# A causal attention block on one core: one decision on the score bound, read behind the tail, in place of one before each chunk with two code paths

## The chip, the core and the metric

The program runs on one core of a Trainium2 chip. The metric is the device time of one execution in microseconds. The core has five engines with an instruction list each: PE (TensorE, matmuls and transposes), DVE (VectorE), ACT (ScalarE), POOL (GpSimd) and SP (SyncE, which issues every DMA here). They meet at semaphores.

## The reference

One transformer block on 2048 tokens of width 256, all in float32:

```python
x = x + attn(layernorm(x))       # 16 heads of 16, causal, softmax over up to 2048 keys, o_proj
x = x + ffn(layernorm(x))
# ffn: x @ W.T + b, plus a LoRA update of rank 16 from the top 2 of 8 experts,
#      picked by x @ gate_w.T + gate_b, weighted by the softmax of the two logits
```

The softmax is exact for any input. The kernel leaves out the subtraction of the row maximum where it can show that no exponential overflows. For that it bounds every score by the largest squared norm of a query head times the largest squared norm of a key head. With the inputs used here the bound always holds, so the general path, with row maxima, is never run in any time of this document.

## The kernel before, in words

The tokens are cut into 16 tiles of 128 and four chunks of 512 queries. TensorE projects q, k and v of each tile. q and k are split into a float16 high and low part, stored to DRAM and loaded back as stacks (`load_queries`, `load_keys`), in which one matmul of 64 rows gives an exact enough score.

The attention is one list of 272 units, each of 128 keys by two halves of 512 queries. A unit is four or fewer score matmuls (`scores_of`, L741), one exponential of ScalarE (L846), and for the diagonal blocks one mask of VectorE (`clear_later_keys`, L1062). Groups of units are multiplied by the values (`values_of`, L758). Chunk c takes units `FIRST_UNIT[c]` on: 0, 20, 72 and 156. Two units and what belongs to them are a step; the chunks begin at steps 0, 10, 36 and 78, and steps 136 and 137 hold only the last four value groups. There are three score banks, so unit u needs the exponential of unit u - 3.

Between the units, `place_pieces` puts the pieces of other work into the steps: the projection of the next chunk's tiles (turn_x, project_qk L612, project_v L618), the norms of the chunk (norm_q, norm_k, L624) and what follows attention for the tiles of earlier chunks (turn_sums to lora, with the FFN at L669). In chunk 0 a step has two slots for pieces, later one. Every engine goes through the same steps in the same order, and a piece on TensorE waits until the bank of the piece before it has been read (`bank_read`). The last four tiles go through `TAIL_ORDER` when attention is over.

The first chunk's projections are outside the loop (`project_first_chunk`). It ends with the norms of chunk 0 on TensorE (`sum_squares`), their maxima on VectorE (`read_norm`), the seven small steps of `decide_bound` (L1006 to L1019, ending in the flag `is_bounded`), and the transpose of tile 4 on TensorE, which waits for one norm read. `decide_bound` runs again in norm_k of each chunk, for chunk c over the norms of all chunks so far.

Before each chunk TensorE, VectorE and SyncE wait for that chunk's decision, load the flag into a register and branch. TensorE's list holds the steps of each chunk twice, once for either path:

```python
bounded = pe.value_load(is_bounded[0:1, c:c + 1], min_val=0, max_val=1)
with pe.If(bounded == 1):
    for s in range(FIRST_STEP[c], FIRST_STEP[c + 1]):
        step(s, False)
with pe.If(bounded == 0):
    ...
        step(s, True)
```

The second block is jumped over at the end of each chunk, chunk 3 included, ahead of steps 136 and 137. SyncE's list in order: the inputs, the stores and stack loads of chunk 0, the loads of the rest (L435 to L441), then per chunk the decision and, at each project_qk, six stores (`store_parts`) and behind the chunk's last tile the 16 stack loads of the next chunk.

Of the kernel before, what the change touches and what calls it, by code (L numbers as in the profile page):

```python
# [37 lines left out]
PAIRS = H // 2  # L38

# [83 lines left out]
def place_pieces():  # L123
# [78 lines left out]
def transformer_block(nc, x, wqkv, wo, wffn, lora_b, biases, ident, masks, head_sum, expert_ids, ones, out):  # L202
    ctx = ExitStack()
    with ctx:
# [6 lines left out]
        def sem(name):  # L211
# [6 lines left out]
        shift_dram = nc.dram_tensor("shift_dram", (NCHUNK, H, TPC, P), F32, kind="Internal").ap()  # L218
# [8 lines left out]
        masks_sb = sb("masks_sb", [P, 2, P])  # L227
# [20 lines left out]
        squares = sb("squares", [P, 2 * KH, CHUNK], BF16)  # L248
# [6 lines left out]
        is_bounded = sb("is_bounded", [1, NCHUNK], I32)  # L255
# [13 lines left out]

        k32 = k_stack[:].rearrange("p c a t -> p (c a t)").bitcast(F32).rearrange("p (i t) -> p i t", t=S)  # L270
        q32 = [q_stack[:, b].rearrange("p a s -> p (a s)").bitcast(F32).rearrange("p (i t) -> p i t", t=CHUNK)
               for b in range(2)]
        row_max = sb("row_max", [P, 8])
        masked = sb("masked", [P, P])
        shift = sb("shift", [P, TPC])
        shift_out = sb("shift_out", [P, TPC])
        shift_rows = sb("shift_rows", [TPC, P])
# [56 lines left out]
        gen_loaded = [sem(f"gen_loaded{c}") for c in range(NCHUNK)]  # L334
        gen_scores = [sem(f"gen_scores{c}") for c in range(NCHUNK)]
        gen_step = [sem(f"gen_step{c}") for c in range(NCHUNK)]
        gen_read = [sem(f"gen_read{c}") for c in range(NCHUNK)]
        gen_max = [sem(f"gen_max{c}") for c in range(NCHUNK)]
        gen_turned = [sem(f"gen_turned{c}") for c in range(NCHUNK)]
        gen_rows = [sem(f"gen_rows{c}") for c in range(NCHUNK)]  # L340
        gen_out = [sem(f"gen_out{c}") for c in range(NCHUNK)]
        gen_pair = [sem(f"gen_pair{c}") for c in range(NCHUNK)]
        gen_in = [sem(f"gen_in{c}") for c in range(NCHUNK)]
# [50 lines left out]
        tail = [AfterAttention(carver(k32[:, t]), True) for t in range(TPC)]  # L394
        tail_banks = [scores[0][:, 0], scores[0][:, 1], scores[1][:, 0], scores[1][:, 1]]
        tail_turn_banks = [scores[2][:, 0, 0:P], scores[2][:, 1, 0:P], aux[:, 0:P], acc[:, 0:P]]

# [3 lines left out]
        def bank_of(g):  # L401
            return aux[:] if g < TILES - TPC else tail_banks[g - (TILES - TPC)]

        def turn_bank_of(g):
            return aux[:, 0:P] if g < TILES - TPC else tail_turn_banks[g - (TILES - TPC)]

        def sums_of_tile(g, q):
            t = g % TPC
            return sums[:, g // TPC % 3, q, t * P:(t + 1) * P]

# [12 lines left out]
        def _(sp):  # L423
# [6 lines left out]
            sp.dma_start(masks_sb[:], masks).then_inc(consts_in, 16)  # L430
# [55 lines left out]
            def load_general(c):  # L486
                sp.wait_ge(first_qk32_out, 16 * 2 * KH)
                if c > 0:
                    sp.wait_ge(scores_ready, FIRST_UNIT[c])
                    for b in range(2):  # L490
                        sp.wait_ge(qk32_out[b], 16 * 2 * c)
                rows = qk32_dram.rearrange("c k m (j d a) t -> c k m j d a t", j=2, d=DK)
# [33 lines left out]
            for c in range(NCHUNK):  # L526
# [13 lines left out]
                for s in range(FIRST_STEP[c], FIRST_STEP[c + 1]):  # L540
                    for slot in range(2):
# [12 lines left out]
                        if name == "lora":  # L554
                            store_result(n)
# [728 lines left out]
```

## Time and profile before

| | us |
|---|---|
| median of 3 runs (lowest, highest) | 413.61 (411.25, 413.66) |
| the profiled execution | 415.72 |
| its span, first to last instruction | 413.9 |
| busy: PE, ACT, DVE, POOL | 363.4, 279.8, 213.3, 47.8 |
| mean granted clock of TensorE | 0.950 of full |
| scores of chunk 0, 1, 2, 3 begin | 24.15, 71.58, 141.70, 245.46 |
| last value groups begin | 383.36 |

The profile comes from one execution. Times are microseconds from the start of the span. In the timeline an entry is a run of like instructions: when it starts, how long it takes, how many, and in brackets how long its engine was idle before it and what released it. "issue" means that the profile shows nothing that the engine waited for. The granted clock is a share of TensorE's full 2.4 GHz; 0.50 is its lower level.

### The profile page before, as it was taken

How to read it: one execution, taken by the hardware profiler on the slowest of the kernel's cores; microseconds unless marked ns; L12 is line 12 of the kernel's file. 1: busy time of each engine (PE TensorE's matmuls, PEld its weight loads, DVE VectorE, ACT ScalarE, POOL GpSimd, SP SyncE). 2: the span in 40 equal slices, each digit the busy share in tenths (PEclk: the TensorE clock that was granted, in tenths of full speed). 3: DMA queues.
4: the chain of work that ended last, by engine and by line, in shares of the span. 5: the costliest groups of instructions: out<-in, count | busy, mean ns of one | idle time of the engine just before them, and what ended most of it. 6: DMA issues, size and time to landing. Idle time of an engine off the chain costs nothing.

```text
span 413.9 us, 7036 instructions
## 1 busy us (share of the span) xinstructions
PE 363.4 (88%) x2558; PEld 142.1 (34%) x2558; DVE 213.3 (52%) x734; ACT 279.8 (68%) x317; POOL 47.8 (12%) x75
## 2 busy tenths in 40 slices
PE   7966975899998799999999979998997999797884
PEld 3544621445332254423323223233322323211542
DVE  4647565354766535555555444546446344402385
ACT  2524345767887777788788856888787588799121
POOL 5000100001011100011121111211121111100050
PEclk9988869899999999999999999999999899899896
DMA  6578335022350021261000000000000000000001
GB/s 197 159 253 258 82 103 157 18 60 78 89 169 13 3 53 51 74 194 52 14 1 15 13 5 13 2 14 0 14 13 2 13 2 13 14 0 4 3 1 51
DMA packets 29390, 23.51 MB, mean 57 GB/s; under 512 B 15392, under 2 KB 25888, under 8 KB 29344
## 3 DMA queue, kind: packets, MB, share of 16 engines
q1 hardware_dynamic: 29344, 22.91, 18.6%
q8 instruction: 28, 0.46, 0.5%
q14 instruction: 18, 0.15, 0.1%
HBM read 12.41 MB, written 10.49 MB: 55 GB/s over the span
## 4 chain that ended last, share of the span: by engine, by line
PE 63%; DVE 18%; issue 8%; ACT 8%; POOL 2%; DMA 1%; ACTq 0%; DVEq 0%
PE acc L758 23%; PE scores L741 12%; PE aux L612 7%; ACT probs L846 7%; PE aux L669 5%; PE aux L653 3%; PE aux L682 2%; DVE probs L1062 2%; PE aux L618 2%; PE aux L638 1%; DVE ffn L1109 1%; POOL exp_gap L1217 1%; DVE parts L977 1%; DVE gates L1137 1%; PE aux L661 1%
## 5 line engine op out<-in xcount | busy, mean ns | idle before, releaser
L846 ACT ACTIVATE probs<-scores 128x1024 f32<-128x1024 f32 x272 | 260.5, 1031 | 86.1 <-PE scores L741 74.9
L758 PE MATMUL acc<-probs,v_aug 128*32 128x512 f32 (+3 forms) x1280 | 149.5, 555 | 3.3 <-DVE probs L1062 2.4
L741 PE MATMUL scores<-q_stack,k_stack 64*128 64x512 f16 (+3 forms) x640 | 87.3, 357 | 15.6 <-issue 12.1
L741 PEld LDWEIGHTS scores<-q_stack,k_stack 64*128 64x128 f16 x640 | 21.1, 95 | 116.5 <-ACT probs L846 78.8
L1062 DVE TENSOR_TENSOR probs<-probs,masks_sb 128x512 f32<-128x512 f32 (+1 forms) x80 | 44.2, 579 | 23.9 <-ACT probs L846 23.3
L758 PEld LDWEIGHTS acc<-probs,v_aug 128*32 128x32 f32 x1280 | 31.8, 111 | 54.6 <-issue 34.9
L612 PE MATMUL aux<-xT,wqkv_sb 128*128 128x128 f32 x192 | 28.8, 311 | 1.0 <-DVE xT L964 1.0
L612 PEld LDWEIGHTS aux<-xT,wqkv_sb 128*128 128x128 f32 x192 | 26.4, 221 | 5.7 <-issue 3.2
L975 DVE CAST parts<-qk 128x512 f16<-128x512 f32 x12 | 5.1, 427 | 39.9 <-ACT qk L838 39.9
L1206 POOL TENSOR_TENSOR rstd<-ve,minus_half 128x1 f32<-128x1 f32 x12 | 7.3, 608 | 112.2 <-DVE ve L955 112.2
L669 PE MATMUL aux<-wffn_sb,yT 128*128 128x392 f32 x48 | 20.0, 543 | 0.0
L1211 POOL TENSOR_TENSOR rstd<-ve,minus_half 128x1 f32<-128x1 f32 x12 | 6.6, 549 | 106.3 <-DVE ve L1093 106.3
L1109 DVE COPY ffn<-aux 128x392 f32<-128x392 f32 x12 | 6.8, 567 | 22.8 <-PE aux L669 22.8
L1086 DVE TENSOR_TENSOR y<-aux,x_sb 128x256 f32<-128x256 f32 x12 | 5.1, 425 | 23.9 <-PE aux L653 23.9
L1217 POOL TENSOR_TENSOR exp_gap<-euler,top_gap 128x1 f32<-128x1 f32 x12 | 6.6, 550 | 90.3 <-DVE top_gap L1122 90.3
L1067 DVE COPY sums<-acc 128x512 f32<-128x512 f32 x16 | 11.0, 687 | 10.3 <-PE acc L758 10.2
L618 PE MATMUL aux<-wqkv_sb,xT 128*128 128x256 f32 x48 | 13.6, 405 | 1.2 <-ACT qk L838 1.0
L1159 DVE TENSOR_TENSOR result<-aux,yb 128x256 f32<-128x256 f32 x12 | 5.1, 425 | 17.7 <-PE aux L682 17.7
L1098 DVE TENSOR_SCALAR yln<-y,mv,rstd 128x256 f32<-128x256 f32 x12 | 9.7, 810 | 8.0 <-POOL rstd L1211 8.0
L653 PE MATMUL aux<-wo_sb,attn_t 128*128 128x256 f32 x48 | 13.6, 405 | 0.0
L838 ACT COPY qk<-aux 128x512 f32<-128x512 f32 x12 | 7.0, 585 | 9.4 <-PE aux L612 9.4
L676 PE MATMUL aux<-ident_sb,gated 128*128 128x128 f32 x12 | 3.9, 326 | 9.1 <-DVE attn_t L1080 8.2
(148 smaller groups left out, 328.1 us busy)
## 6 DMA issues: line engine op xcount, KB each, us to landing
q_stack<-q_dram SPq DMA_DIRECT2D x32, 128.0 KB, 2.8
k_stack<-k_dram SPq DMA_DIRECT2D x32, 128.0 KB, 2.8
qk_dram<-qk SPq DMA_DIRECT2D x12, 256.0 KB, 2.5
x_sb<-x SPq DMA_DIRECT2D x3, 512.0 KB, 6.8
q_dram<-parts SPq DMA_DIRECT2D x12, 128.0 KB, 2.0
k_dram<-parts SPq DMA_DIRECT2D x48, 32.0 KB, 1.9
out<-result SPq DMA_DIRECT2D x12, 128.0 KB, 1.7
qk_dram<-probs SPq DMA_DIRECT2D x4, 256.0 KB, 3.4
```

Of the source, the lines that this page charges most:

```text
L612: m = pe.matmul(aux[:, n * P:(n + 1) * P], wqkv_sb[:, k, col:col + P], xT[:, k, :], start=(k == 0), stop=(k == KH - 1))
L618: m = pe.matmul(aux[:, 0:D], xT[:, k, :], wqkv_sb[:, k, 2 * D:3 * D], start=(k == 0), stop=(k == KH - 1))
L653: m = pe.matmul(bank_of(g)[:, 0:D], w.attn_t[:, k, :], wo_sb[:, k, :], start=(k == 0), stop=(k == KH - 1))
L669: m = pe.matmul(bank_of(g)[:, 0:FFN], w.yT[:, k, :], wffn_sb[:, k, :], start=(k == 0), stop=(k == KH - 1), skip_group_check=True)
L741: m = pe.matmul(to, k_stack[row:row + STACK, kb // TPC, 2 * i + p, kb % TPC * P:(kb % TPC + 1) * P], q_stack[row:row + STACK, c % 2, 2 * i ...
L758: m = pe.matmul(acc[32 * hp:32 * hp + 32, lo:CHUNK], v_aug[:, kb, QUAD * i + hp, :], probs[:, u % PROBS, hp % 2, col:col + CHUNK - lo], st ...
L846: act.activation(probs[:, u % PROBS], scores[u % BANKS][:], ACT.Exp, scale=EXP_SCALE).then_inc(exp_done, 1)
L1062: dve.tensor_tensor(tile, tile, mask, ALU.min).then_inc(causal_done, 1)
L1067: dve.tensor_copy(sums[:, c % 3, i, :], acc[:]).then_inc(acc_read, 1)
L1098: dve.tensor_scalar(w.yln, w.y, w.mv2[:, 0:1], w.rstd2, ALU.subtract, ALU.mult).then_inc(yln_ready, 1)
L1109: dve.tensor_copy(w.ffn, bank_of(g)[:, 0:FFN]).then_inc(ffn_ready, 1)
L1217: pool.tensor_tensor(w.exp_gap, euler[:], w.top_gap, ALU.pow).then_inc(gap_exp, 1)
```

## The change

The decision is made once, at norm_k of the last chunk, over all four chunks. All chunks run the bounded path with no branch. Behind the tail every engine loads the flag and jumps over one general block, or runs it; it computes all of attention and the FFN anew in loops. The norms of chunk 0 leave `project_first_chunk` and become two pieces in chunk 0, ahead of norm_q and norm_k of chunk 1; for that `squares` gets a second buffer, and tile 4's transpose no longer waits for a norm read. The second half of the mask tensor (128x128) goes, a 1x1 memset is added at the start. The functions of the pieces take the tile number and the buffers as arguments, so that the general loop can call them; what they issue for a tile is the same.

```diff
@@ place_pieces
-            pre += [("norm_q", c + 1), ("norm_k", c + 1)]
             if c == 0:
                 pre.remove(("turn_x", TPC))
+                pre += [("norm_q", 0), ("norm_k", 0)]
+            pre += [("norm_q", c + 1), ("norm_k", c + 1)]
@@ SyncE
-            for c in range(NCHUNK):
-                sp.wait_ge(bound_step, BOUND_STEPS * (c + 1))
-                bounded = sp.value_load(is_bounded[0:1, c:c + 1], min_val=0, max_val=1)
-                with sp.If(bounded == 0):
...
-                    load_general(c)
-                    store_shifts(c)
...
+            for s in range(QK_STEPS):
+                for slot in range(2):
+                    name, n = PIECE_AT.get((s, slot), (None, None))
+                    if name == "project_qk":
+                        store_parts(n)
...
             for t in range(TPC):
                 store_result(TILES - TPC + t)
+            sp.wait_ge(bound_step, BOUND_STEPS)
+            bounded = sp.value_load(is_bounded[0:1, 0:1], min_val=0, max_val=1)
+            with sp.If(bounded == 0):
+                general()
@@ TensorE
                 pe.wait_ge(consts_in, 16 * 2)
-                pe.wait_ge(squared, 2 * KH)
-                pe.wait_ge(first_qk32_ready, 2)
-                for a in range(2):
-                    sum_squares(0, a, first_banks[a])
-                pe.wait_ge(norm_read, 1)
+                pe.wait_ge(first_qk32_ready, 1)
                 turn_x(TPC)
...
-            for c in range(NCHUNK):
-                if c == 1:
+            for s in range(STEPS):
+                if s == FIRST_STEP[1]:
                     pe.wait_ge(post_weights_in, 16 * 5)
-                pe.wait_ge(bound_step, BOUND_STEPS * (c + 1))
-                bounded = pe.value_load(is_bounded[0:1, c:c + 1], min_val=0, max_val=1)
-                with pe.If(bounded == 1):
-                    for s in range(FIRST_STEP[c], FIRST_STEP[c + 1]):
-                        step(s, False)
-                with pe.If(bounded == 0):
...
-            for s in range(QK_STEPS, STEPS):
-                step(s, False)
+                step(s)
             pe.wait_ge(exp_done, len(UNITS))
...
+            pe.wait_ge(bound_step, BOUND_STEPS)
+            bounded = pe.value_load(is_bounded[0:1, 0:1], min_val=0, max_val=1)
+            with pe.If(bounded == 0):
+                general()
@@ VectorE
+                dve.memset(hold_cell[:], 0.0).then_inc(gen_divided, 1)
...
-                for a in range(2):
-                    read_norm(0, a, first_banks[a])
-                decide_bound(0)
                 store_xT(TPC)
...
             def norm_k(c):
-                read_norm(c, 1, aux[:])
-                decide_bound(c)
+                read_norm(c, 1)
+                if c == NCHUNK - 1:
+                    decide_bound()
```

VectorE loses its branches in the same way; it, ScalarE and GpSimd get the load and the jump of the flag at their end.

## Rows read from the trace of the kernel before

**Rows 1.** The page, part 1: busy us, share of the span and instructions of each engine.

```profile
PE 363.4 (88%) x2558; PEld 142.1 (34%) x2558; DVE 213.3 (52%) x734; ACT 279.8 (68%) x317; POOL 47.8 (12%) x75
```

**Rows 2.** Stretches view, chunk 2: busy PE, PEld, DVE, ACT, POOL; granted clock; DMA; GB/s.

```profile
141.60:245.40 103.80, 98.59 (x744) 36.27 (x744) 55.03 (x185) 82.90 (x88) 11.62 (x19) 1.00 0.17 47
```

**Rows 3.** The list of waits: engine, line, releaser, us in total, times, longest.

```profile
PE scores L741 <- issue: 12.1, 4, 4.1
```

**Rows 4.** Timeline of TensorE, start: start us, us, line, operation, idle before and its releaser.

```profile
19.75 0.59 PE L624 MATMUL acc<-squares,head_sum_sb 128*16 128x512 bf16 x2
24.15 0.71 PE L741 MATMUL scores<-q_stack,k_stack 64*128 64x512 f16 x4 [2.65 <-issue]
24.79 3.54 PE L612 MATMUL aux<-xT,wqkv_sb 128*128 128x128 f32 x16
...
32.61 2.02 PE L612 MATMUL aux<-xT,wqkv_sb 128*128 128x128 f32 x16 [0.65 <-DVE xT L964]
```

**Rows 5.** Timeline of TensorE, the start of chunk 1.

```profile
71.58 0.61 PE L741 MATMUL scores<-q_stack,k_stack 64*128 64x512 f16 x4 [4.07 <-issue]
72.59 1.10 PE L741 MATMUL scores<-q_stack,k_stack 64*128 64x512 f16 x4
73.62 3.04 PE L612 MATMUL aux<-xT,wqkv_sb 128*128 128x128 f32 x16
```

**Rows 6.** Timeline of TensorE, the start of chunk 2.

```profile
141.70 0.61 PE L741 MATMUL scores<-q_stack,k_stack 64*128 64x512 f16 x4 [2.56 <-issue]
```

**Rows 7.** Timeline of TensorE, the start of chunk 3 and a later stretch of it.

```profile
245.46 0.61 PE L741 MATMUL scores<-q_stack,k_stack 64*128 64x512 f16 x4 [2.86 <-issue]
246.00 2.63 PE L669 MATMUL aux<-wffn_sb,yT 128*128 128x392 f32 x4
248.56 1.66 PE L758 MATMUL acc<-probs,v_aug 128*32 128x512 f32 x8
...
262.42 1.07 PE L758 MATMUL acc<-probs,v_aug 128*32 128x512 f32 x8
263.96 1.58 PE L669 MATMUL aux<-wffn_sb,yT 128*128 128x392 f32 x4
```

**Rows 8.** Timeline of TensorE, the last value groups.

```profile
383.36 4.67 PE L758 MATMUL acc<-probs,v_aug 128*32 128x512 f32 x32 [2.40 <-DVE probs L1062]
```

**Rows 9.** Timeline of VectorE, the masks of units 268 and 271.

```profile
379.55 0.43 DVE L1062 TENSOR_TENSOR probs<-probs,masks_sb 128x256 f32<-128x256 f32 x1 [0.49 <-ACT probs L846]
...
382.29 0.69 DVE L1062 TENSOR_TENSOR probs<-probs,masks_sb 128x512 f32<-128x512 f32 x1 [0.22 <-ACT probs L846]
```

**Rows 10.** Timeline of VectorE, the start.

```profile
20.01 0.41 DVE L959 TENSOR_SCALAR xln<-x_sb,mv,rstd 128x256 f32<-128x256 f32 x1 [0.67 <-POOL rstd L1206]
...
22.74 0.14 DVE L1019 TENSOR_SCALAR is_bounded<-bound_max 1x1 int32<-1x1 f32 x1
```

**Rows 11.** SyncE's timeline and the landing times of line 457, the first key loads.

```profile
17.03 1.97 SPq L457 DMA_DIRECT2D k_stack<-k_dram  x4
...
DMA to landing us min/median/max: 2.8/2.9/3.3
```

**Rows 12.** Timeline of ScalarE, the end of chunk 0.

```profile
63.07 5.63 ACT L846 ACTIVATE probs<-scores 128x1024 f32<-128x1024 f32 x6 [1.27 <-PE scores L741]
```

**Rows 13.** Timeline of TensorE, the norms in chunk 0.

```profile
55.98 1.02 PE L624 MATMUL aux<-squares,head_sum_sb 128*16 128x512 bf16 x2 [2.65 <-DVE v_aug L988]
```

**Rows 14.** Timeline of SyncE, after the constant loads and at the end.

```profile
32.90 0.65 SPq L441 DMA_DIRECT2D expert_ids_sb<-expert_ids  x1
34.97 0.39 SPq L474 DMA_DIRECT2D q_dram<-parts  x1
...
409.40 2.71 SPq L484 DMA_DIRECT2D out<-k_stack  x4
```

**Rows 15.** Timeline of VectorE, the start of chunk 2 and the last result.

```profile
142.71 0.43 DVE L964 COPY xT<-aux 128x256 f32<-128x256 f32 x1 [2.39 <-PE aux L604]
...
411.32 0.42 DVE L1159 TENSOR_TENSOR k_stack<-scores,k_stack 128x256 f32<-128x256 f32 x1 [0.43 <-PE scores L682]
```

More of the change, by code:

```diff
@@ L515, in _ @@
+                with sp.Fori(0, TILES) as i:
+                    sp.wait_ge(result_ready, TILES + i + 1)
+                    sp.dma_start(out[bass.ds(i, 1)].rearrange("o p d -> (o p) d"), loop[0].result
+                                 ).then_inc(result_out[0], 16)
+                sp.wait_ge(result_out[0], 16 * (TILES // 2 + TILES))
             for m in range(KH):
@@ L770, in step, with general @@
                 piece(s, 1)
+            def general():
+                with pe.Fori(0, H) as h:
+                    with pe.Fori(0, TILES) as g:
+                        n = TILES * h + g
+                        pe.wait_ge(gen_q_ready, n + 1)
+                        for c in range(NCHUNK):
+                            m = pe.matmul(scores[c // 2][:, c % 2, :], gen_q_tile, gen_k[:, c * CHUNK:(c + 1) * CHUNK],
+                                          start=True, stop=True)
+                        m.then_inc(gen_scores, 1)
+                        pe.wait_ge(gen_exp, n + 1)
+                        for kb in range(TILES):
+                            m = pe.transpose(scores[kb // 8][:, kb // 4 % 2, kb % 4 * P:(kb % 4 + 1) * P],
+                                             gen_probs[:, kb * P:(kb + 1) * P], ident_sb[:])
+                        m.then_inc(gen_turned, 1)
+                        pe.wait_ge(gen_copied, n + 1)
+                        for kb in range(TILES):
+                            m = pe.matmul(acc[:, 0:32], gen_probs_t[:, kb * P:(kb + 1) * P], gen_v[:, kb, :],
+                                          start=(kb == 0), stop=(kb == TILES - 1))
+                        m.then_inc(gen_summed, 1)
+                with pe.Fori(0, TILES) as i:
+                    for name in POST_PIECES[1:]:
+                        POST[name](TILES + i, loop[0])
@@ L1165, in _, with store_gatedT, finish @@
-            LATER = {"o": normalise_y, "ffn": gate_inputs}
+            def store_gatedT(n, w):
+                dve.wait_ge(gatedT_psum, n + 1)
+                dve.tensor_copy(w.gatedT, w.turn_bank).then_inc(gatedT_ready, 1)
+            def finish(n, w, parity, stored):
+                dve.wait_ge(out_psum, n + 1)
+                if w.in_tail:
+                    dve.wait_ge(yb_ready, n + 1)
+                else:
+                    dve.wait_ge(base_ready, counted(n) + 1)
+                    if stored is not None:
+                        dve.wait_ge(result_out[parity], stored)
+                dve.tensor_tensor(w.result, w.bank[:, 0:D], w.yb, ALU.add).then_inc(result_ready, 1)
@@ L1202, in _ @@
+            bounded = dve.value_load(is_bounded[0:1, 0:1], min_val=0, max_val=1)
+            with dve.If(bounded == 0):
+                general()
         @block.gpsimd
@@ L1269 @@
         "ident": np.eye(P, dtype=np.float32),
-        "masks": np.stack([np.where(row[None, :] >= row[:, None], BIG, 0.0),
-                           np.where(row[None, :] <= row[:, None], BIG, -BIG)], 1).astype(np.float32),
+        "mask": np.where(row[None, :] >= row[:, None], BIG, 0.0).astype(np.float32)[:, None, :],
         "head_sum": np.stack([head_of[:, None] + m * (P // DK) == np.arange(H)[None, :] for m in range(KH)],
@@ L1274 @@
         "expert_ids": np.broadcast_to(np.arange(E, dtype=np.float32)[None], (P, E)).copy(),
-        "ones": np.ones((1, NQUAD, S), np.float32),
+        "band": np.where(np.arange(2 * S - P)[None, :] - (S - P) <= row[:, None], BIG, -BIG).astype(np.float32),
     }
```

524 lines of the change are left out of this document (244 added, 280 removed).

## The prediction, made before the result was known

> **What bounds the kernel now.** I read the page's busy shares first: TensorE is busy 88% of the span, ScalarE 68%, VectorE 52% [rows 1]. The granted clock and busy time by stretch come next: in the undisturbed chunk 2 TensorE is busy 98.6 of 103.8 us at full clock, ScalarE 82.9 [rows 2]. So the attention loop is bound by TensorE, which runs its list in order, and a pause of TensorE there is lost time unless ScalarE has to catch up behind it. The list of waits then says where TensorE pauses with nothing in the profile to wait for: the scores line has four such pauses, 12.1 us together, the longest 4.1 [rows 3]. The timeline of TensorE places them: 2.65 us before the first scores [rows 4], 4.07 before chunk 1 [rows 5], 2.56 before chunk 2 [rows 6], 2.86 before chunk 3 [rows 7]. These are the four places where the kernel loads the decision and branches. A fifth branch, over the general code of chunk 3, stands before the last value groups; there TensorE pauses 2.40 us [rows 8]. The profile names VectorE's mask as the releaser because that one came last, but the first of the groups needs only the mask of unit 268, done at 379.55 + 0.43 = 379.98 [rows 9], while TensorE was free at 383.36 - 2.40 = 380.96. So this pause too is the branch.
>
> **The start.** Today the first scores wait for the first chunk's norms, the seven decision steps (the flag is written at 22.74 + 0.14 = 22.88 [rows 10]) and 1.27 us more for load and branch, until 24.15 [rows 4]. Without that, what is late next is the key stack. Its four loads are issued from 17.03 to 19.00, the last of them about 0.4 us before that, and a load lands in 2.8 to 3.3 us [rows 11]: 21.4 to 21.9. I take 21.7; the x tile's transpose (its tile is normalised at 20.01 + 0.41 = 20.42 [rows 10], and it no longer waits for the norm read) isn't later. Saving 24.15 - 21.7 = 2.45 us, between 2.2 and 2.75.
>
> **The boundaries.** For chunk 1 TensorE would be free at 71.58 - 4.07 = 67.51, but ScalarE's six exponentials, one each 0.94 us, end at 68.70 [rows 12], and a score bank comes free three units later: the fourth unit of the chunk needs the exponential of the first, at 69.7. The first projection then starts at about 70.0 and not at 73.62 [rows 5]: 3.6 us. At chunks 2 and 3 ScalarE is not behind, and I take the pauses whole, 2.56 and 2.86 [rows 6, 7]. At the end, the first group starts at 380.96; the last one waits for the last mask, at 382.29 + 0.69 = 382.98 [rows 9]. Taking only the pause: 2.40. Sum of pauses: 2.45 + 3.6 + 2.56 + 2.86 + 2.40 = 13.9 us. Because TensorE finds all of ScalarE's work done after a pause and will not without one, I give 1.0 of it back to small new waits (0 to 3).
>
> **The clock behind the pauses.** After four of the five pauses the same work takes longer. The 16 projection matmuls take 3.54 us behind the first pause and 3.04 behind the second, 2.02 elsewhere [rows 4, 5]: 1.5 and 1.0 us, and the four score matmuls ahead of the second take 1.10 for some 0.6 [rows 5], another 0.5. Behind the pause of chunk 3 the FFN takes 2.63 for 1.58 and a value group 1.66 for 1.07 [rows 7]: 1.6 us. The last 32 value matmuls take 4.67 us, where 8 at full width take 1.07 [rows 7, 8]; they cover 512 + 384 + 128 + 256 columns, that is 2.5 times one group, 2.7 us, so 1.9 are lost. This is TensorE at the lower of its clocks, 1.2 GHz for 2.4, after an idle stretch; behind the 2.56 us pause it didn't fall [rows 2]. With no pause, TensorE is busy throughout at the last three, so I count 1.5 + 1.6 + 1.9 = 5.0 in full, and the first, where small idle pieces remain, at half: 0.75. Sum 5.75, between 0 and 6.5.
>
> **What is added.** The norms of chunk 0 become two pieces in chunk 0. One piece is a pair of these matmuls, 0.59 us at the start [rows 4] and 1.02 at the lower clock in chunk 0 [rows 13], so 1.2 to 2.0 for both pieces; their two reads on VectorE replace the decision steps that leave that place. The pieces follow the projection of the chunk's last tile, so no stack load is behind them; they delay the last exponentials of chunk 0. I take 1.2, since ScalarE paces the end of chunk 0 and covers part; 3 if each also waits for VectorE's read. The other two decisions deleted, the halved mask load and one 1x1 memset lie beside other work: VectorE is half idle [rows 1] and the memset precedes the first x load. If that cover were gone, the memset would add one short instruction. SyncE no longer stops 1.4 us after the constant loads (33.55 to 34.97 [rows 14]) and issues the stores of chunk 0's projections sooner; these are needed again only two tiles later, so nothing is counted.
>
> **The end.** All five engines now load the flag and jump over the general code. PE, ACT and POOL are done earlier than VectorE, whose last result is at 411.32 + 0.42 = 411.74 [rows 15]; SyncE issues the last store until 409.40 + 2.71 = 412.11 [rows 14] and then waits out its landing, up to the end of the span, 413.9, which covers its own 1.4 us. The profile has no jump of VectorE at the end; at chunk 2 one, with its load, fits in the 2.39 us before 142.71 [rows 15]. That gives 414.1 at most, 0.2 over the present end; by TensorE's longest pause, 4.07, it would be 1.9. Below nothing it cannot be, as instructions are only added. I take 0.5.
> The Trainium skill's "Runtime: NRT & Kernel Launch" (Instruction fetch mechanics) says that a taken branch whose target lies outside the two pages at hand must fetch by DMA before going on. The row on TensorE agrees in kind; VectorE's and SyncE's jumps at the end pass over less code and could by that rule be free. "Advanced Engine Details and Errata" (Control Flow Timing) gives a compare-and-branch as about 108 ns: by it alone the end term would be 0.1 and the sum 0.4 larger, but the boundary pauses of [rows 6, 7] are over twenty times that figure.
>
> **The sum.** 13.9 - 1.0 + 5.75 - 1.2 - 0.5 = 16.95 us. Against the profiled execution's own 415.72 (1.8 of it outside the span of 413.9, taken as unchanged): 398.8. That execution is 2.1 over the median of 413.61, from which the same sum gives 396.7. I predict 398.0, nearer the former since the sum was made there. This case by itself reaches from 394 to 402.
>
> **Rivals.**
> Clock stays low: the pauses go but the falls happen elsewhere (chunk 0 has idle stretches of over 2 us from VectorE anyway). The sum is 13.9 - 1.0 - 1.7 = 11.2, so 404.5 (402.4 by the median). For it: in chunk 0 the norm matmuls of [rows 13] are at the lower clock with no branch near them. Against: chunk 2 at 1.00 [rows 2]. Chance 0.17.
> Pauses refilled: ScalarE, the mask or the stack loads end the wait in their place, half the pauses stay: 7.0 - 1.7 with some 2 of clock is 7.3, so 408.4. For it: 68.70 for ScalarE at chunk 1. Against: chunks 2 and 3, where it is idle about as long as TensorE. Chance 0.10.
> The pauses are not the branch: TensorE's code has to be fetched anyway at these places and only the start is saved, 2.45 + 0.75 - 1.7 = 1.5: 414.2, no change. This is also the case in which the change doesn't do what it says. Against it: all four unexplained pauses of the line stand at chunk starts and none inside chunk 2 with its 744 matmuls [rows 2, 3]. Chance 0.05.
> Slower: the five jumps at the end, each off the straight code, are served one after the other and each costs TensorE's worst, 4.07: 20.4 us behind the last result, 398.8 - 0.5 + 20.4 = 418.7, and 424 if the clock stays low. It decides from 3.5 us a jump upward, if serial. Against: POOL, ScalarE and TensorE are done before VectorE, so that their jumps overlap the tail. Chance 0.03, of which 0.01 stays within the bound below.
> The forecast itself has 0.65.
>
> **Range and chances.** The forecast's case, the clock rival and the bounds of the added terms (413.61 less 13.9 and 6.5, plus 1.2 for the norms and nothing at the end, is 394.4; the start could give 0.3 more, and the runs before spread by 2.4) make 392.5 to 406; above that lies about half of the second rival and the two others. A measurement of this kernel tells about 1% from no change, 4.1 us. Faster by more: 0.65 + 0.17 + 0.10 = 0.92; within: 0.05 + 0.01 = 0.06; slower: 0.02.
>
> **What would show it.** In the changed profile TensorE has no pause over 1 us labelled issue in front of the scores of chunks 1 to 3; the first scores start at 21.4 to 22; the stretch of chunk 3 begins about 13 us sooner; the last value groups take under 3.3 us from first to last start, with the clock at 1.0; four pairs of norm matmuls stand in chunk 0; and the last instruction of VectorE is within 2.5 us of the last result. Wrong would be: pauses of the same length still there, first scores waiting past 23, projection (or FFN) matmuls behind the chunk starts still at half clock, or over 3 us of bare issue after the last store.

## The result, and the profile after

The changed kernel takes 393.35 us (median of 4, 393.10 to 393.75), the kernel before 412.71 (median of 4, 411.25 to 413.66): ratio 0.9535, 95% interval 0.9498 to 0.9571. That is 19.4 us faster. In a later comparison it was 394.19 (median of 6) against 413.54, ratio 0.9518, interval 0.9477 to 0.9559. The forecast was 398.0, with a range of 392.5 to 406. The direction, the mechanism and the range held; the forecast gave 76% of the gain, 14.7 of 19.4 us.

The profiled execution took 393.18 us, its span 391.4. The page, busy shares and granted clock in 40 slices:

```profile
PE 354.2 (90%) x2558; PEld 138.0 (35%) x2558; DVE 209.7 (54%) x711; ACT 279.5 (71%) x317; POOL 47.8 (12%) x75
...
PEclk9997969999999999999999999999999999999997
```

TensorE is busy 90% of the span [rows 1: 88%]; in the slices the clock falls visibly only in chunk 0 (slices 4 and 6) and in the last slice, behind attention. The timeline of TensorE shows the start, the norm pieces and the start of chunk 1:

```profile
20.61 0.41 PE L588 MATMUL aux<-ident_sb,xln 128*128 128x128 f32 x2 [1.18 <-DVE xln L936]
21.68 0.61 PE L696 MATMUL scores<-q_stack,k_stack 64*128 64x512 f16 x4 [0.66 <-issue]
22.21 2.05 PE L596 MATMUL aux<-xT,wqkv_sb 128*128 128x128 f32 x16
...
51.90 1.02 PE L608 MATMUL aux<-squares,head_sum_sb 128*16 128x512 bf16 x2 [2.65 <-DVE v_aug L965]
58.46 0.59 PE L608 MATMUL aux<-squares,head_sum_sb 128*16 128x512 bf16 x2
60.04 0.60 PE L608 MATMUL aux<-squares,head_sum_sb 128*16 128x512 bf16 x2 [0.45 <-DVE norms L970]
64.09 0.79 PE L696 MATMUL scores<-q_stack,k_stack 64*128 64x512 f16 x4
66.64 2.05 PE L596 MATMUL aux<-xT,wqkv_sb 128*128 128x128 f32 x16
```

Against [rows 4]: the first scores are at 21.68 in place of 24.15, and the first projection takes 2.05 us and not 3.54. The norms are now four pairs, two more than before. By the order of the pieces the norms of chunk 0, the added ones, are the first two (at 51.90 and, not shown, at 53.82); those of chunk 1 follow at 58.46 and 60.04. Against [rows 5], the scores of chunk 1 follow with no idle time, 7.49 us earlier, and the projection takes 2.05 and not 3.04. The starts of chunks 2 and 3 and the last value groups:

```profile
130.09 1.07 PE L713 MATMUL acc<-probs,v_aug 128*32 128x512 f32 x8
131.09 0.61 PE L696 MATMUL scores<-q_stack,k_stack 64*128 64x512 f16 x4
...
231.93 0.61 PE L696 MATMUL scores<-q_stack,k_stack 64*128 64x512 f16 x4
232.46 1.58 PE L651 MATMUL aux<-wffn_sb,yT 128*128 128x392 f32 x4
233.98 1.06 PE L713 MATMUL acc<-probs,v_aug 128*32 128x512 f32 x8
...
361.38 1.92 PE L713 MATMUL acc<-probs,v_aug 128*32 128x512 f32 x16
363.70 1.56 PE L713 MATMUL acc<-probs,v_aug 128*32 128x384 f32 x24 [0.40 <-DVE probs L1010]
```

The pauses of [rows 6, 7, 8] are gone: a value group ends at 131.16 and the next scores are in its tail at 131.09. The FFN takes 1.58 us and a value group 1.06. Ahead of the last mask TensorE still waits 0.40 us, but the first of the last groups is done by then, and none of them runs at the lower clock any more. By stretches (chunk 0 from 24, chunks 2 and 3; us, then busy PE, PEld, DVE, ACT, POOL, granted clock, DMA share, GB/s):

```profile
24.00:64.09 40.09, 31.63 (x238) 16.83 (x237) 25.40 (x63) 18.39 (x22) 2.00 (x3) 0.83 0.68 202
...
131.09:231.93 100.84, 98.54 (x749) 36.25 (x746) 54.73 (x186) 83.10 (x89) 11.62 (x19) 1.00 0.17 48
231.93:360.54 128.61, 119.71 (x873) 35.41 (x871) 56.22 (x206) 107.34 (x114) 16.22 (x26) 1.00 0.03 8
```

Chunk 2 is 100.84 long against 103.80 [rows 2], with TensorE's busy time unchanged at 98.5 us: that chunk lost its 2.9 us pause and nothing else. In the list of waits the entry of [rows 3] has shrunk from 12.1 us to one wait of 0.7, the 0.66 before the first scores. The largest entry for these matmuls is now

```profile
PE scores L696 <- ACT probs L814: 2.0, 6, 0.5
```

The end, VectorE's last result and SyncE's last stores:

```profile
388.55 0.42 DVE L1104 TENSOR_TENSOR k_stack<-scores,k_stack 128x256 f32<-128x256 f32 x1 [0.43 <-PE scores L662]
```

```profile
386.63 2.70 SPq L491 DMA_DIRECT2D out<-k_stack  x4
```

The last result is at 388.97 and the span ends at 391.4, 2.4 us behind it; before it was 413.9 - 411.74 = 2.2 [rows 15].

How the gain of this pair of executions adds up, each from the times of the same instructions in both (the shift grows by the difference at each place):

| place | shift before it | shift behind it | gives | forecast |
|---|---|---|---|---|
| first scores | 0 | 2.47 | 2.47 | 2.45 |
| first projection (clock) | 2.47 | 4.08 | 1.61 | 0.75 |
| added norm pieces, to the end of chunk 0 | 4.08 | 3.35 | -0.73 | -1.2 |
| chunk 1, pause (to the first projection) | 3.35 | 6.98 | 3.63 | 3.6 |
| chunk 1, clock of that projection | 6.98 | 7.97 | 0.99 | 1.5 |
| chunk 2, pause | 7.97 | 10.61 | 2.64 | 2.56 |
| chunk 3, pause | 10.61 | 13.53 | 2.92 | 2.86 |
| chunk 3, clock behind it | 13.53 | 15.18 | 1.65 | 1.6 |
| inside chunk 3 | 15.18 | 18.51 | 3.33 | 0 |
| last value groups, pause and clock | 18.51 | 22.76 | 4.25 | 4.3 |
| end | 22.76 | 22.5 | -0.3 | -0.5 |
| new small waits | | | 0 | -1.0 |

The 3.33 us inside chunk 3 stand at no branch. In the profile of before the clock fell twice in mid-chunk (TensorE alone; us, busy, granted clock, DMA, GB/s), where in this profile of after it stays at 1.00 throughout:

```profile
315.00:323.00 8.00, 5.71 (x53) 0.91 0.00 1
323.00:331.00 8.00, 8.00 (x50) 0.88 0.05 16
355.00:363.00 8.00, 6.94 (x54) 0.79 0.06 18
```

The first fall follows a wait of 2.29 us for `attn_t`, which the changed kernel has too, with 1.94; the 0.35 us between them are part of the 3.33. The changed kernel has these falls as well, in other executions. In its second profile, of an execution of 394.70 us, they are back at the same two places:

```profile
PEclk9998989999999999999999999999999899899996
```

From the first scores of chunk 3 to the last value group ahead of the last four that profile takes 132.30 us (230.60 to 362.90) and the first one 129.45 (231.93 to 361.38), so the two falls cost 2.85 us there. Five of the fourteen profiles kept have both falls: before, the second one of the changed kernel, and those with far branches, with the load alone and without the end; three have one of them and six none. They are one of the ways in which executions of one kernel differ. The profiled execution of before, 415.72, lay 3 us over the median of 412.71.

### The profile page after: what moved, and what is told of

It is laid out like the page before. It is cut to its first block, busy times and chain, and to the rows that moved or that the text cites. A ratio compares the mean times of both kernels' runs of the same rounds, so it can differ in the third digit from the quotient of the medians.

```text
span 391.4 us, 6977 instructions
## 1 busy us (share of the span) xinstructions
PE 354.2 (90%) x2558; PEld 138.0 (35%) x2558; DVE 209.7 (54%) x711; ACT 279.5 (71%) x317; POOL 47.8 (12%) x75
## 4 chain that ended last, share of the span: by engine, by line
PE 63%; DVE 20%; ACT 7%; issue 6%; POOL 2%; DMA 1%; DVEq 0%; ACTq 0%
PE acc L713 23%; PE scores L696 12%; PE aux L596 7%; ACT probs L814 6%; PE aux L651 5%; PE aux L637 3%; DVE probs L1010 2%; PE aux L662 2%; PE aux L602 2%; PE aux L623 1%; DVE ffn L1055 1%; POOL exp_gap L1216 1%; PE aux L644 1%; DVE gates L1083 1%; DVE parts L954 1%
## 5 line engine op out<-in xcount | busy, mean ns | idle before, releaser
L713 PE MATMUL acc<-probs,v_aug 128*32 128x512 f32 (+3 forms) x1280 | 145.4, 545 | 1.3 <-ACT probs L814 0.9
L1010 DVE TENSOR_TENSOR probs<-probs,mask_sb 128x512 f32<-128x512 f32 (+1 forms) x80 | 44.2, 577 | 22.5 <-ACT probs L814 22.0
L713 PEld LDWEIGHTS acc<-probs,v_aug 128*32 128x32 f32 x1280 | 30.8, 110 | 49.8 <-issue 29.7
L596 PE MATMUL aux<-xT,wqkv_sb 128*128 128x128 f32 x192 | 26.3, 294 | 1.0 <-DVE xT L941 1.0
L596 PEld LDWEIGHTS aux<-xT,wqkv_sb 128*128 128x128 f32 x192 | 24.0, 203 | 5.4 <-issue 3.1
L651 PE MATMUL aux<-wffn_sb,yT 128*128 128x392 f32 x48 | 19.0, 518 | 0.0
L602 PE MATMUL aux<-wqkv_sb,xT 128*128 128x256 f32 x48 | 13.6, 405 | 1.2 <-ACT qk L806 1.0
L637 PE MATMUL aux<-wo_sb,attn_t 128*128 128x256 f32 x48 | 13.6, 405 | 0.0
L1104 DVE TENSOR_TENSOR result<-aux,yb 128x256 f32<-128x256 f32 x12 | 5.1, 425 | 14.7 <-PE aux L662 14.7
```

Of the source, the lines that this page charges most:

```text
L596: m = pe.matmul(aux[:, n * P:(n + 1) * P], wqkv_sb[:, k, col:col + P], xT[:, k, :], start=(k == 0), stop=(k == KH - 1))
L602: m = pe.matmul(aux[:, 0:D], xT[:, k, :], wqkv_sb[:, k, 2 * D:3 * D], start=(k == 0), stop=(k == KH - 1))
L637: m = pe.matmul(w.bank[:, 0:D], w.attn_t[:, k, :], wo_sb[:, k, :], start=(k == 0), stop=(k == KH - 1))
L651: m = pe.matmul(w.bank[:, 0:FFN], w.yT[:, k, :], wffn_sb[:, k, :], start=(k == 0), stop=(k == KH - 1), skip_group_check=True)
L713: m = pe.matmul(acc[32 * hp:32 * hp + 32, lo:CHUNK], v_aug[:, kb, QUAD * i + hp, :], probs[:, u % PROBS, hp % 2, col:col + CHUNK - lo], st ...
L1010: dve.tensor_tensor(tile, tile, mask, ALU.min).then_inc(causal_done, 1)
```

## The experiments

All versions are made from the changed kernel. The ratio is always to the kernel before, run on the same chip between them. The versions with far and near branches, with the load alone and with the old start ran together (before: 413.80), then those with pauses, without the end, with late norms and with the first reordering (413.56), then the other four (413.54). Their yardstick is the changed kernel: 0.9535 in its first runs, 0.9518 beside the last ones.

**The branches put back.** TensorE's list gets the form of the old one:

```diff
+            for c in range(1, NCHUNK):
...
+                taken = pe.value_load(always[0:1, 0:1], min_val=0, max_val=1)
+                with pe.If(taken == 1):
+                    for s in range(FIRST_STEP[c], FIRST_STEP[c + 1]):
+                        step(s)
+                with pe.If(taken == 0):
+                    for s in range(FIRST_STEP[c], FIRST_STEP[c + 1]):
+                        step(s)
```

> The changed kernel, with TensorE's branches put back at the starts of chunks 1, 2 and 3 and nothing else: it loads a flag that is always 1, runs the chunk's steps under one branch and jumps over a second copy of the same steps (also ahead of the last value groups). No decision is waited for. If the pauses are the load and the jump over much code: 2.5 to 4.1 us without a releaser in front of the scores of chunks 1 to 3 and 2 to 2.4 ahead of the last value groups, 10.5 to 11.5 us together, plus up to 5 of clock: 404 to 409 us, against 393.35. If the pauses came from the decision or from code that has to be fetched anyway: 393 to 395.

Measured: 408.19 us (404.51 to 410.80), ratio 0.9852, interval 0.9773 to 0.9931: some 13 us of the gain are gone again. The profile is of its slowest execution, 410.80. Of the timeline of TensorE, the starts of chunks 1, 2 and 3 and the last value groups:

```profile
64.50 0.73 PE L698 MATMUL scores<-q_stack,k_stack 64*128 64x512 f16 x4
...
134.25 0.61 PE L698 MATMUL scores<-q_stack,k_stack 64*128 64x512 f16 x4 [2.74 <-issue]
136.98 1.04 PE L698 MATMUL scores<-q_stack,k_stack 64*128 64x512 f16 x4
137.95 2.39 PE L598 MATMUL aux<-xT,wqkv_sb 128*128 128x128 f32 x16
...
240.05 0.61 PE L698 MATMUL scores<-q_stack,k_stack 64*128 64x512 f16 x4 [3.27 <-issue]
240.59 2.53 PE L653 MATMUL aux<-wffn_sb,yT 128*128 128x392 f32 x4
...
377.91 3.88 PE L715 MATMUL acc<-probs,v_aug 128*32 128x512 f32 x32 [2.64 <-DVE probs L1024]
```

The pauses are back, 2.74, 3.27 and 2.64 us, with no decision to wait for; and behind them work at the lower clock (scores 1.04, FFN 2.53, value groups 3.88). At the start of chunk 1 there is no pause, because in this version nothing is jumped over there: it only loads the flag and falls into the block. My expectation named chunk 1 too; that was an error in reading my own edit, and it turned out to be the cleanest row of the run. The load and a branch not taken cost nothing there.

The profile also counts what the engines fetch as code. Of the page's part on DMA queues, the line of queue 8 (packets, MB, share), before, after, and with a short jump, a jump of middle length and far branches (the next versions):

```profile
q8 instruction: 28, 0.46, 0.5%
...
q8 instruction: 21, 0.34, 0.4%
...
q8 instruction: 22, 0.36, 0.4%
...
q8 instruction: 26, 0.43, 0.5%
...
q8 instruction: 27, 0.44, 0.5%
```

A packet is 16 KB. The versions with branches differ from the changed kernel in TensorE's list and one small memset only, so the 1, 5 and 6 added packets are TensorE's code; every other version has 21. In the trace the packets of the changed kernel start at least 13.6 us apart. In each of the four pauses behind a jump before the change, the three here and the two long ones with the middle jump, one starts 1.0 us before to 0.6 us after TensorE runs dry, and the next one 3.0 to 3.5 us later. At the seven chunk starts among them the scores begin 3.3 to 3.7 us after the first of the two has started. So the pause is a wait for code, and its length is what is left of this time when TensorE's queued work has run out: the 2.56 us ahead of chunk 2 had its packet start 1.04 us before that (138.10 to 139.14), the 4.07 us ahead of chunk 1 only 0.56 us behind it (67.51 to 68.07).

Not all of the time lost lies in the pauses. The span ends 3.4 us behind the last result here, where the changed kernel has 2.4, and 3.4 and 3.7 us in the versions with a short and a middle jump. In these three the last packet of queue 8 starts between 0.2 us before and 0.7 us behind the end of the last result, in the changed kernel 7.9 us before it. So about 1 us of each of these versions is lost at the end, and not at the chunk starts; which code that last packet holds the profile doesn't say.

**A short jump.** As above, with `step(FIRST_STEP[c])` alone in the second block.

> As the version with far branches, but the block jumped over holds one step only in place of the chunk's 26 to 58 steps. If the cost is the fetch behind a far jump: what is left is the load, 1.3 us at each of three chunk starts, and almost nothing ahead of the last value groups, 397 to 398 us, with no fall of the clock. If a taken branch costs its price whatever it passes over: pauses and time as with the far branches, 404 to 409.

Measured: 394.75 us (393.75 to 396.71), ratio 0.9572, interval 0.9502 to 0.9643. The start of chunk 2:

```profile
130.51 0.61 PE L698 MATMUL scores<-q_stack,k_stack 64*128 64x512 f16 x4
```

No pause at any of the three places. So a taken branch as such costs TensorE no visible pause here; what cost 2.6 to 4 us was the fetch behind a long jump. The 1.3 us per load that I expected are not there either.

**The load alone.** `pe.value_load(always...)` at the starts of chunks 1 to 3, no branch.

> The changed kernel with only the flag's load put back on TensorE at the starts of chunks 1 to 3, no branch. If the load costs what the start of the old kernel showed behind the decision (22.88 to 24.15): three pauses of about 1.2 us, 396.5 to 397.5 us. If the load is the larger part of the old pauses of 2.56 to 4.07: over 2 us each, 399.5 or more. If only branches cost: 393.5.

Measured: 394.57 us (393.14 to 396.31), ratio 0.9562, interval 0.9490 to 0.9634. The first scores and the start of chunk 2:

```profile
21.75 0.61 PE L698 MATMUL scores<-q_stack,k_stack 64*128 64x512 f16 x4 [0.68 <-DMA k_stack<-k_dram]
...
128.51 0.61 PE L698 MATMUL scores<-q_stack,k_stack 64*128 64x512 f16 x4
```

The load doesn't show. Both that expectation and the 1.3 us in the one before it were wrong. The likely reason, which no row shows by itself, is that the load of a flag already set passes while matmuls issued before it still run. The first row is a gift: here the profile names what the first scores wait for, the landing of the key stack, as the prediction had it.

**A jump of middle length**, 10 steps of the chunk in the second block.

> As the versions with far and near branches, the block jumped over being the first 10 steps of the chunk (far: all 26 to 58; near: 1). If the price is a fetch that begins once the target lies some way behind the code at hand, and 10 steps are within it: no pause and the time of the near version, 394 to 395. If 10 steps are beyond it: pauses of 2.6 to 3.3 us at the start of chunks 2 and 3 and ahead of the last value groups, 404 to 409. If the price grows with the distance: pauses of about 1 us, 397.

Measured: 405.96 us (401.25 to 407.27), ratio 0.9774, interval 0.9716 to 0.9832. TensorE at the same three places:

```profile
134.18 1.03 PE L698 MATMUL scores<-q_stack,k_stack 64*128 64x512 f16 x4 [2.81 <-issue]
...
240.95 0.61 PE L698 MATMUL scores<-q_stack,k_stack 64*128 64x512 f16 x4 [3.24 <-issue]
...
375.51 1.88 PE L715 MATMUL acc<-probs,v_aug 128*32 128x512 f32 x25 [1.40 <-issue]
```

The two pauses have their full size, 2.81 and 3.24 us, with 10 steps to pass over in place of 26 and 42. So at these two places the price doesn't grow with the distance; between 1 and 10 steps lies a limit behind which it is whole. At the last place it is 1.40, in the middle of the last value groups, with the first of them already done; there the same 10 steps cost less, so the number of steps is not all that counts.

**Pauses without a branch.** GpSimd, which is idle, waits for the chunk's last value matmul and then holds TensorE at the four places for about the time of the old pauses (7, 4, 5 and 4 operations):

```diff
+                pool.wait_ge(pv_done, done)
+                for k in range(PAUSES[c]):
+                    at = sum(PAUSES[b] for b in range(1, c)) + k
+                    p = pool.tensor_tensor(pause_cells[:, at:at + 1], euler[:], minus_half[:, 0:1], ALU.pow)
+                p.then_inc(paused, 1)
...
+                if s in FIRST_STEP[1:]:
+                    pe.wait_ge(paused, FIRST_STEP.index(s))
```

> The changed kernel, no branch put back; TensorE is held at the starts of chunks 1, 2, 3 and ahead of the last value groups until GpSimd, set off by the last value matmul before, has done 7, 4, 5 and 4 small operations of 0.55 us (3.9, 2.2, 2.8 and 2.2 us, the lengths of the old pauses). If a pause costs its length and the lower clock behind it: 3.5 + 2.3 + 2.9 + 2.3 = 11 of pause and 0 to 5 of clock, 404 to 409 us, and behind the pauses the projection, FFN and value matmuls take up to double. If the slow matmuls behind the old pauses came from the jump itself (code that arrives slowly): 404 with the clock at 1.0 behind the pauses.

Measured: 412.01 us (median of 10, 410.62 to 415.08), ratio 0.9981, interval 0.9939 to 1.0023. This gives back the whole gain with no branch in the list. TensorE at the four places:

```profile
66.66 1.04 PE L698 MATMUL scores<-q_stack,k_stack 64*128 64x512 f16 x4 [3.97 <-issue]
69.22 3.61 PE L598 MATMUL aux<-xT,wqkv_sb 128*128 128x128 f32 x16
...
137.91 1.04 PE L698 MATMUL scores<-q_stack,k_stack 64*128 64x512 f16 x4 [2.62 <-POOL pause_cells L1240]
142.32 2.93 PE L598 MATMUL aux<-xT,wqkv_sb 128*128 128x128 f32 x16
...
244.67 0.61 PE L698 MATMUL scores<-q_stack,k_stack 64*128 64x512 f16 x4 [2.99 <-POOL pause_cells L1240]
245.20 1.58 PE L653 MATMUL aux<-wffn_sb,yT 128*128 128x392 f32 x4
...
379.73 4.01 PE L715 MATMUL acc<-probs,v_aug 128*32 128x512 f32 x32 [3.01 <-POOL pause_cells L1240]
```

The pauses are 3.97, 2.62, 2.99 and 3.01, 12.6 us together. The time rose by some 18, by the ratios, so another 5 to 6 went to the clock and to what it delayed: behind the first pause the projection takes 3.61 us, behind the second 2.93, and the last value groups 4.01 for 32 matmuls. Two things follow. The slow matmuls behind the old pauses need no code that arrives slowly: the lower clock behind idle time gives them by itself. And which pause brings the clock down is not fixed by its length: here the one of 2.62 did and the one of 2.99 didn't, in [rows 6, 7] it was the other way round. I was wrong on the size of the sum only: I had 409 as its upper end.

**The old start alone.** Norms of chunk 0 and a decision ahead of the loop; TensorE waits for it, without load or branch; no norm pieces of chunk 0 in the loop.

```diff
+                for a in range(2):
+                    sum_squares(0, a, first_banks[a])
+                pe.wait_ge(norm_read, 1)
...
+            pe.wait_ge(bound_step, BOUND_STEPS)
             for s in range(STEPS):
```

> The changed kernel with the start of the old one: chunk 0's norms and a decision ahead of the loop, TensorE waits for the decision before its first scores but neither loads nor branches; the norm pieces of chunk 0 are gone from chunk 0. By my steps: first scores at about 22.95 in place of 21.68 (+1.3 us), less the norm pieces (-0.7 to -1.2), and if the clock falls behind the wait another 1.5: 393.5 to 395.5. If the whole 2.47 us at the start came from the wait for the decision: first scores at 24.1 and 395 or more.

Measured: 392.32 us (median of 5), ratio 0.9497, interval 0.9417 to 0.9577; three executions at 392.24 to 392.32, two at 398.5. My 393.5 to 395.5 was missed by both groups. So in time this run is inconclusive: at its best it is 1 us below the changed kernel and not above it, and the two groups lie 6 us apart. Its profile is of one of the late ones, in which the first projections ran at the lower clock and everything up to here is 1.67 us later. Within it the distance from the flag to the scores can be read, VectorE and then TensorE:

```profile
24.41 0.14 DVE L1004 TENSOR_SCALAR is_bounded<-bound_max 1x1 int32<-1x1 f32 x1
```

```profile
24.65 0.74 PE L699 MATMUL scores<-q_stack,k_stack 64*128 64x512 f16 x4 [1.48 <-DVE is_bounded L1004]
25.32 3.51 PE L599 MATMUL aux<-xT,wqkv_sb 128*128 128x128 f32 x16
```

From the flag's end, 24.55, to the scores are 0.10 us; before the change it was 22.88 to 24.15, 1.27. So at the start, where the flag was fresh and TensorE's sequencer stood waiting for it, load and branch did cost 1.17 us. The same load and untaken branch are free at the start of chunk 1 in the version with far branches and 1.17 us here. Two things differ, the flag's age and the matmuls still queued on TensorE; that the price shows when nothing is queued behind which it can hide is my reading, and no run separates the two.

**The end alone**: all five loads, branches and the general block left out.

> The changed kernel without the flag's loads, the branches and the general block at the end of all five lists (the general path is left out). If the end costs what I put on it: 392.9, between 391.5 and 393.35, with the span ending within 2.2 us of the last result as before the change. If the jumps at the end are hidden: no difference from the changed kernel, 393.35, and from its 2.43 us behind the last result.

Measured: 395.25 us (393.29 to 397.18), ratio 0.9558, interval 0.9476 to 0.9641. No gain, by the medians 1.9 us more, where I had expected 391.5 to 393.35. In its profile the last result is at 390.96 and the span ends at 393.2, 2.2 us behind it, against 2.4 in both profiles of the changed kernel. By that the jumps at the end cost 0.2 us here, and queue 8 has 21 packets with and without them. The three versions with branches, 3.4 to 3.7 us, show that this isn't so wherever TensorE's last code lies.

**The norms of chunks 2 and 3 moved to the end of chunk 3**, as two lines of `place_pieces`:

```diff
-            pre += [("norm_q", c + 1), ("norm_k", c + 1)]
+            if c == 0:
+                pre += [("norm_q", 1), ("norm_k", 1)]
...
+    late = [(name, c) for c in (2, 3) for name in ("norm_q", "norm_k")]
```

> The changed kernel with the norm pieces of chunks 2 and 3 (four pairs of matmuls) moved from chunks 1 and 2, where TensorE sets the time, to the free steps behind the last FFN pieces in chunk 3, where ScalarE does. A pair takes 0.43 to 0.59 us of TensorE. If they lie on the path where they are now and are hidden there: 4 times 0.45 = 1.8 us less, 391.5. If ScalarE or VectorE sets the time around them: no change, 393.35.

Measured: 395.37 us (394.91 to 397.51), ratio 0.9576, interval 0.9500 to 0.9652: no gain, by the medians 2 us more. The four pairs did land where nothing waits for them. But the pieces behind them moved up by two steps in chunk 1 and four in all, into other neighbours (TensorE now waits 1.08 us for `attn_y` at one transpose in chunk 1). The run doesn't separate the two effects; this question stays open.

**VectorE's order in chunk 0.** In the changed kernel's profile TensorE still waits 2.65 us for `v_aug` before the norms (as in [rows 13]), because VectorE does two masks first.

```diff
+                first = s < FIRST_STEP[1] and name in ("project_v", "turn_x")
+                if first:
+                    after_piece(name, n)
                 for u in (2 * s - 2, 2 * s - 1):
...
-                if (s, 0) in PIECE_AT:
-                    name, n = PIECE_AT[s, 0]
+                if name is not None and not first:
                     after_piece(name, n)
```

> The changed kernel, in which VectorE in chunk 0 does the turn_x and project_v pieces of a step ahead of its masks and not behind them. TensorE waits 2.65 us for v_aug behind two masks before its norm pieces (and 2.6 us before that at tile 7's transpose). If the masks ahead are what holds it: 1.2 us less at each of two places and perhaps one fall of the clock fewer, 389 to 391. If the masks are then missed by the value groups: no change.

Measured: 391.47 us (390.82 to 392.04), ratio 0.9469, interval 0.9399 to 0.9540, a little above the 389 to 391 that I expected. The three runs that settle it, on one chip, in five rounds:

> The changed kernel once more, on the same chip and in the same rounds as the three below, as their yardstick. By its first runs: 393.1 to 393.8 us; if its clock falls once more or once less in chunk 0 than in those, 392 to 396, which would say that one execution's place in that span is chance.

> The version in which VectorE, in chunk 0, stores the v tile and the turned x tile ahead of a step's masks. Its profile has TensorE wait 1.45 us for v_aug before the norms in place of 2.65. If that is a gain of the order of the wait: 1.5 to 2.5 us under the changed kernel beside it. If the first comparison was chance of clock or chip: within 1 us of it.

> VectorE does every piece except project_qk ahead of the step's masks, in all chunks and not only in chunk 0. If the pieces are what TensorE waits for also in chunks 1 to 3 (it waits up to 0.9 us for single ones there): another 0.5 to 2 us below the version with chunk 0 only. If the masks are then late for the value groups of the diagonal blocks: above it by 1 us or more.

| version | us, median of 6 | lowest, highest | ratio to before | 95% interval |
|---|---|---|---|---|
| the changed kernel | 394.19 | 393.18, 395.16 | 0.9518 | 0.9477, 0.9559 |
| reordered in chunk 0 | 391.97 | 389.97, 393.52 | 0.9464 | 0.9418, 0.9511 |
| reordered in all chunks | 391.49 | 390.88, 392.72 | 0.9460 | 0.9420, 0.9499 |

Both are 2.2 and 2.7 us below the changed kernel by the medians. For the second all six executions lie below its lowest; the intervals of the ratios overlap a little, since they carry the spread of the kernel before. The reordering beyond chunk 0 gives nothing that can be told. TensorE's two waits for `v_aug` in the version with chunk 0 only, and the place where the rest of the gain went, ScalarE's copy of q and k of tile 6:

```profile
34.25 0.44 PE L588 MATMUL aux<-ident_sb,xln 128*128 128x128 f32 x2 [1.38 <-DVE v_aug L965]
51.69 0.60 PE L608 MATMUL aux<-squares,head_sum_sb 128*16 128x512 bf16 x2 [1.45 <-DVE v_aug L965]
```

```profile
41.72 0.59 ACT L806 COPY qk<-aux 128x512 f32<-128x512 f32 x1 [4.67 <-DMA qk_dram<-qk]
```

The waits are 1.38 and 1.45 us, where they were 2.6 each. From the first scores to those of chunk 1 it is 40.19 us (22.21 to 62.40) in place of 42.41 (21.68 to 64.09). Part of that is the clock, which in this stretch falls once, and in the changed kernel's first profile twice and for longer. The copy now waits 4.67 us for the store of tile 4's q and k, from the same buffer; in the changed kernel it waited 2.46:

```profile
40.68 0.59 ACT L806 COPY qk<-aux 128x512 f32<-128x512 f32 x1 [2.46 <-DMA qk_dram<-qk]
```

SyncE issues that store only after the loads of the constants. I had counted nothing for it, as "needed again only two tiles later"; with chunk 0 some 4 us earlier, as in both these versions, that no longer holds. Putting these loads behind tile 4's stores wasn't tried.

## Why the prediction was right, step by step

**The pauses are the branches**: right. The first four came out within 0.1 us of the forecast (2.47, 3.63, 2.64, 2.92 against 2.45, 3.6, 2.56, 2.86). That also answers the rival by which the pauses belong to the code and not the branch: with the branches back they are back, with a short jump they are not. What was imprecise is "load and branch". At the chunk starts the load is free and all of the pause is the long jump; at the start of the loop, where nothing is jumped over, the 1.17 us are load and a branch not taken. I took the length of a pause as a property of its branch; it depends on how long before or behind TensorE's last queued work the packet of code starts. The rule of the Trainium skill's "Runtime: NRT & Kernel Launch" (Instruction fetch mechanics), a stall for a DMA fetch where the target of a taken branch isn't in the two pages at hand, agrees with the three lengths of jump: at the chunk starts nothing, 2.8 to 3.2 and 2.7 to 3.3 us, with 1, 5 and 6 more packets of code. No run shows where its pages end.

**The fifth pause, that the profile puts down to a mask**: right, 4.25 us for pause and clock against 4.3. The reason it could be seen was the order of the groups: the last wait named isn't the wait that the first group needed.

**The clock**: right in kind, 0.5 too much at chunk 1. There I had counted the slow scores ahead of the projection twice, once as part of the 3.6 and once by themselves. At the start I took half of 1.5 and it was 1.61, by luck of the execution as much as by the change: in four of the other profiles with the new start the clock falls to its lower level between 22.1 and 22.8 us, with no branch ahead of it. The experiment with pauses and no branch shows that this part is the price of the idle time itself.

**The refund of 1.0 for new small waits**: wrong, it was nothing. ScalarE's slack in chunks 2 and 3 was real, and at chunk 1 I had already paid for it.

**The norm pieces**: 0.73 and not 1.2, since ScalarE's lateness covered part of them. **The end**: 0.3 and not 0.5.

**The sum.** Mine is 16.95, these two executions differ by 22.5 and the medians by 19.4. The execution of before contained the 3.33 us inside chunk 3 that the one of after didn't; without them the two differ by 19.2, which is what the medians say. So of the 4.65 us between 398.0 and 393.35 about half, 2.4, are the terms: 1.0 for small waits that didn't come, 0.9 of clock at the start, 0.5 for the norm pieces and 0.2 for the end, less 0.5 of clock at chunk 1, and for the rest tenths at the pauses and between executions and medians. 1.3 more are the choice of the base: I set the forecast nearer to the profiled 415.72 than to the median of 413.61, by which the same sum gives 396.7, though the forecast is compared with medians. The last 0.9 is that this median itself came out at 412.71.

**The rivals**: the clock did not stay low; the pauses were not refilled; and the jumps at the end were not served one after the other (0.2 us for all five). The pauses did belong to the branches. In chunk 0 the clock does still fall, 0.83 over the stretch, as the first rival said of that place.

## What to carry to other kernels

Look in the list of waits for pauses that nothing explains and see whether they stand where the program jumps. Here one long jump cost 2.6 to 3.3 us of TensorE, and with the lower clock behind it often half as much again, while a jump over one step, a branch not taken, and the load of a flag set long before cost TensorE no pause at a chunk start. So a rare path belongs behind the end of the common one, and not beside it. All of this was measured on TensorE; the branches of VectorE and SyncE were not put back by themselves. The count of code packets on the page is the quickest way to see whether a jump has to fetch. When a sum is made on one profiled execution that lies above its median, find first what in it is peculiar to it, and forecast from the median.

## What the runs showed of the hardware that I had not expected

A pause without any branch costs about the same as one with it: 12.6 us of held TensorE made the kernel some 18 us slower, and with far branches 8.65 us of pauses made it some 13 slower, 1.0 of that at the end. The clock answers to idle time without regard to its reason, but not to its length alone: 2.62 us brought it down at one place and 2.99 did not at another, in the same execution.

How often the clock falls goes with most of the difference between executions of one kernel. The version with the old start came out at 392.3 three times and at 398.5 twice, with mean granted clocks of 0.984 and 0.966; the kernel before ranged from 409.44 at 0.975 to 419.50 at 0.939. A single execution is therefore no measure of a change under 3 us here, whereas the differences between like places of two profiles, where the clock is at the same level in both, came within 0.1 us of the forecast pauses.
